# Two steps' value rows weighed by one VectorE instruction, the products written over the keys, and the mark of a chunk's first node made by ScalarE, in a fused graph-attention stage on one core

## The chip, the cores and the metric

The kernel runs on one core of a Trainium2 chip, as one program. The metric is the device time of one execution in microseconds (us). Before the change the median of three runs is 5581.06 us, the lowest 5578.73 and the highest 5584.89.

## The reference, cut to what matters

Two layers of a graph network on 6250 nodes and 200,000 edges sorted by destination, 256 features. The first layer is attention over the incoming edges with 8 heads, the second a relational layer. The change touches only the first:

```python
h = maximum(layernorm(x), 0)
Q, K, V = h @ Wq, h @ Wk, h @ Wv                       # (6250, 8 heads, 32)
score = einsum('ehd,ehd->eh', Q[dst], K[src]) / sqrt(32)
score = score + relu(efeat @ W1 + b1) @ W2 + b2        # edge MLP
m = segment_max(score, dst); ex = exp(score - m[dst])
denom = segment_sum(ex, dst)
out = segment_sum((ex / denom[dst])[:, :, None] * V[src], dst)
x = x + out.reshape(n, 256) @ Wo + bo
```

## The kernel before, in words

The program has several stages one after another: index preparation, projections (Q stays in SBUF, rows of keys and values go to DRAM as kv_d), the fused attention stage (function attend), the messages and gates of the second layer, and its gather and sum. attend is the stage of the change.

Edges come in groups of 256 (two slices of 128, one edge a partition each). A step handles one group against one block of 128 nodes; there are 832 steps, cut into chunks of R = 8. Four groups make a quad of the edge MLP; there are 196 quads, so the MLP ends 48 steps before the steps do. One loop body (body(i), written once for each engine) issues 16 steps, or two chunks; u is the position in it, and u % 8 the step within a chunk. Each engine's order is fixed by that body, and engines meet only through semaphores.

What a step s issues in iteration u of the body:

- GpSimd gathers the two slices of key and value rows of the step into one of 16 slots of kv_rows by indirect DMA (L1006), once the slot's earlier step has been summed.
- ScalarE makes, from distances (Abs, then Relu of one minus it), the selection matrix pickT of step s+3 (L1043, L1049) and the destination matrix onehot of step s-11 (L1056 twice, L1063), and takes the MLP's results out of PSUM (L1021, L1026, L1033).
- TensorE runs select for step s+1 (L1143: the queries of its edges into one of two PSUM banks p_q, after the product of step s-1 has been read), in the iterations 0 to 3 of a chunk one part of the softmax work of the chunk before (score L1155, L1157; up L1162, L1163; down L1167 to L1169; turn_drop L1174), then its part of the MLP (L1122, L1131, L1115; none in iterations 3 and 7), then add_up of step s-12 (L1183: the segment sums of the weighed value rows).
- VectorE runs dot for step s (L1233 multiplies queries and keys into the tile prod, L1238 sums them by head into dots), put in iteration 7 (L1288), then in iterations 0, 1 and 2 one part of the softmax work (scans L1246, L1248; chain L1264 to L1281, ten short instructions on one partition; drop L1294 to L1302), then weigh of step s-11 (L1308: 2 x 264 value elements times the edge's weight by head, in place) and add of step s-12 (L1326: the sums added to the accumulator; before the first of a chunk also rescale, L1316).

The online softmax runs once a chunk: running maxima along the chunk's edges (scans), carried over its steps (chain), subtracted from the scores (drop), turned back to one edge a partition (turn_drop), exponentiated by ScalarE into wgt and scale (weights, L1070 and L1073, in iteration 3). From then on, from iteration 3 of one chunk to iteration 2 of the next, the eight steps are weighed and summed. first_node (L1266) marks, on one partition, which of 128 nodes is the chunk's first; down multiplies it with fall to spread the fall of the maximum.

hold (L62) is a semaphore wait followed by an increment of a counter on the same engine. The constants LATE = R + 3 = 11 and the body's order set all these distances.

Of the kernel before, what the change touches and what calls it, by code (L numbers as in the profile page):

```python
# [16 lines left out]
ALU = mybir.AluOpType  # L17
ACT = mybir.ActivationFunctionType
AX = mybir.AxisListType

P = 128
# [767 lines left out]
LATE = R + 3  # L789
PICKS = 4  # L790
HOTS2 = 2
PASSES = STEPS // SLOTS


def attend(nc, t, q, att, edge_attr, w1, b1, w2, b2, kv_d, mlp_d, dstrow_d, pens_d, line_d, src_d):
    ctx, sb, ps, sem = phase(nc)
    RH = R * H
    with ctx:
# [14 lines left out]
        rows = sb("kv_rows", [P, SLOTS, 2, KV])  # L813
        prod = sb("prod", [P, 2, D])
        dots = sb("dots", [P, 2, 2, R, H])
# [14 lines left out]
        newmax = sb("newmax", [1, H])  # L830
        fall = sb("fall", [1, H])
        first_node = sb("first_node", [1, P])
        ends = sb("ends", [RH, 2])
        wgt = sb("wgt", [P, 2, 2, R, H])
        scale = sb("scale", [P, H])
# [41 lines left out]
        line_done = sem("line_done")  # L877
        line_down = sem("line_down")
        ends_link = sem("ends_link")
        drop_done = sem("drop_done")  # L880
# [137 lines left out]
        def _(act):  # L1018
# [47 lines left out]
            def weights(c, x):  # L1066
                act.wait_ge(drop_turned, c + 1)
                if not first(c):
                    act.wait_ge(scaled, c)
                nc.scalar.activation(scale[:, :], p_scale, ACT.Exp).then_inc(scale_ready, 1)  # L1070
                if not (isinstance(c, int) and c < 2):
                    act.wait_ge(weighed, R * (c - 1))
                nc.scalar.activation(wgt[:, x, :, :, :].rearrange("p k r h -> p k (r h)"),  # L1073
                                     p_back.rearrange("p (k e) -> p k e", k=2), ACT.Exp).then_inc(wgt_ready, 1)

            def body(i):
                for u in range(SLOTS):
                    s = SLOTS * i + u
                    m = U * i + u // U
                    c = 2 * i + u // R - 1  # L1080
                    if is_step(s + 3):
                        measure(s + 3, (u + 3) // U % 2, (u + 3) % U, 2 * i + (u + 3) // (2 * U))
                    if is_step(s - LATE):
                        measure_dst(s - LATE)
                    if is_quad(m + 1):
                        if u % U < 2:
                            take_hidden(m + 1, u % U)
                        elif u % U == 2:
                            take_mlp(m + 1)
                    if u % U == 3 and is_quad(m + 2):  # L1090
                        take_ef(m + 2)
                    if is_step(s + 3):
                        pick(s + 3, (u + 3) % PICKS)
                    if is_step(s - LATE):
                        hot(s - LATE, (u - LATE) % HOTS2)
                    if u % R == 3 and is_chunk(c):
                        weights(c, (u // R - 1) % 2)
# [13 lines left out]
        def _(pe):  # L1111
# [36 lines left out]
            def score(c, x):  # L1148
                pe.wait_ge(emlp_in, 16 * (c + 1))
                hold(pe, place_ready, c + 1, pe_go)  # L1150
                hold(pe, dots_done, R * (c + 1), pe_go)
                if not first(c):
# [12 lines left out]
            def down(c):  # L1165
                hold(pe, line_done, c + 1, pe_go)
                nc.tensor.transpose(p_ends[:, 0:1], before[:, :], t["ident"][0:1, 0:1])  # L1167
                nc.tensor.transpose(p_ends[:, 1:2], after[:, :], t["ident"][0:1, 0:1])
# [7 lines left out]

            def add_up(s, u):
                pe.wait_ge(hot_ready, s + 1)
                pe.wait_ge(weighed, s + 1)
                if not (isinstance(s, int) and s < 2):  # L1180
# [6 lines left out]
            def body(i):  # L1187
                for u in range(SLOTS):
# [24 lines left out]
                    if is_step(s - LATE - 1):  # L1213
                        add_up(s - LATE - 1, u - LATE - 1)

# [11 lines left out]
        def _(dve):  # L1227
            def dot(s, u, n, x):
                dve.wait_ge(q_done, s + 1)
                dve.wait_ge(gathered[u], 32 * (n + 1))  # L1230
                if not first(s):
                    dve.wait_ge(dots_done, s)
                nc.vector.tensor_tensor(prod[:, :, :], p_q[u % 2][:, :].rearrange("p (k d) -> p k d", k=2), rows[:, u, :, 0:D],  # L1233
                                        ALU.mult).then_inc(prod_done, 1)
                dve.wait_ge(prod_done, s + 1)
                if u % R == 0 and not (isinstance(s, int) and s < 2 * R):
                    dve.wait_ge(score_done, n * 2 + u // R - 1)
                nc.vector.tensor_reduce(dots[:, x, :, u % R, :], prod[:, :, :].rearrange("p k (h c) -> p k h c", h=H),  # L1238
                                        AX.X, ALU.add).then_inc(dots_done, 1)

# [8 lines left out]

            LINKS = 9  # L1250

            def chain(c, s0):
                def linked(n, scan=False):
                    if scan:
                        hold(dve, link, LINKS * c + n, dve_go)
                    else:
# [8 lines left out]
                nc.vector.tensor_copy(firstmax[:, :, :], by_head(p_line[:, 0:RH])[:, :, ::-1]).then_inc(link, 1)  # L1265
                nc.vector.tensor_scalar(first_node[:, :], t["iota"][0:1, :], t["dst"][0:1, bass.ds(2 * s0, 1)], None,  # L1266
                                        ALU.is_equal).then_inc(link, 1)
                linked(1, True)
                nc.vector.tensor_tensor_scan(flat(carried), line[:, 0:H * (R + 1)], flat(lastmax), -BIG, ALU.add, ALU.max).then_inc(link, 1)
                linked(2, True)  # L1270
                nc.vector.tensor_tensor_scan(flat(onward), line[:, H * (R + 1):H * (2 * R + 1)], flat(firstmax), -BIG, ALU.add, ALU.max).then_inc(link, 1)
                linked(4)
                nc.vector.tensor_tensor(by_head(before[:, :]), carried[:, :, 0:R], pen(136, R), ALU.add).then_inc(link, 1)
                nc.vector.tensor_copy(lastmax[:, :, 0:1], carried[:, :, R:R + 1]).then_inc(link, 1)
                linked(5)
                nc.vector.tensor_tensor(by_head(after[:, :])[:, :, 0:R - 1], onward[:, :, R - 2::-1], pen(144, R - 1),
                                        ALU.add).then_inc(link, 1)
                linked(6)
                nc.vector.tensor_tensor(newmax[:, :], before[:, 0:H], onward[:, :, R - 1], ALU.max).then_inc(link, 1)
                linked(9)  # L1280
                nc.vector.tensor_tensor(fall[:, :], before[:, 0:H], newmax[:, :], ALU.subtract).then_inc(line_done, 1)  # L1281
# [22 lines left out]
            def weigh(s, u, c, x):  # L1304
                if u % R == 0:
                    dve.wait_ge(wgt_ready, c + 1)
                v = rows[:, u, :, D:KV].rearrange("p k (h c) -> p k h c", h=H)
                nc.vector.tensor_tensor(v, v, wgt[:, x, :, u % R, :].unsqueeze(3).to_broadcast([P, 2, H, HD1]), ALU.mult).then_inc(weighed, 1)  # L1308

# [19 lines left out]
            def body(i):  # L1329
                for u in range(SLOTS):  # L1330
# [6 lines left out]
                    if is_chunk(c) and u % R < 3:  # L1337
                        if u % R == 0:
                            scans(c)
                        elif u % R == 1:  # L1340
                            chain(c, R * c)
                        else:
                            drop(c)
                    if is_step(s - LATE):
                        v = u - LATE
# [498 lines left out]
```

## Time and profile before

| | |
|---|---|
| median of 3 runs | 5581.06 us (5578.73 to 5584.89) |
| profiled execution, device time | 5578.26 us |
| its span, first to last instruction | 5576.5 us |
| mean granted TensorE clock | 0.878 |
| busy over the span: PE / DVE / ACT / POOL | 4808.8 / 3500.7 / 3299.5 / 3249.0 us |
| the same, share | 86% / 63% / 59% / 58% |
| L1308 (weigh) | 832 instructions, 693 ns mean, 576.5 us |
| L1233 (product), L1238 (head sums) | 832 each, 681 and 686 ns mean |
| L1266 (first_node) | 104 instructions, 265 ns mean, 27.5 us |

Times in the rows are microseconds from the start of the span unless marked ns. PE is TensorE's matmul, PEld its weight load, DVE is VectorE, ACT is ScalarE, POOL is GpSimd. "Busy" is the union of an engine's records in a stretch. Records of neighbouring instructions overlap: one starts while the one before still finishes, so the room that an instruction takes on its engine is the distance to the next start, which is shorter than its duration. An idle time stands in brackets at the end of a timeline line, with what ended it. fp32 matmuls are recorded as two instructions each. The names shelf and p_soft stand for SBUF and PSUM areas that several tiles share: L1326's shelf is the accumulator att, p_soft holds the scores and the small results beside them.

### The profile page before, as it was taken

Reading aid. Unit: us, or ns where it says so; the run is one execution under the profiler, and the core shown is the slowest. Engines: PE = TensorE matmul, PEld = TensorE weight load, DVE = VectorE, ACT = ScalarE, POOL = GpSimd, SP = SyncE. Lnnn points to the kernel's source line nnn. Section 1 sums busy time; section 2 is a strip of 40 time slices with the busy share of each in tenths; the row PEclk is TensorE's granted clock in tenths of the full one; section 3 lists DMA queues with packets and bytes.
Section 4 is the critical chain, followed back from the end, with each engine's and each line's share of the span. In section 5 each row is a group of like instructions: output and inputs, shape, how many; then the busy total and the mean of one; then the engine's idle time right before and its main releaser. Section 6 shows DMA issues by size and latency. Waiting matters only on the chain. (4 is left out here: it accounts for less than half of the span.)

```text
span 5576.5 us, 110596 instructions
## 1 busy us (share of the span) xinstructions
PE 4808.8 (86%) x21476; PEld 2762.5 (50%) x21477; DVE 3500.7 (63%) x8094; ACT 3299.5 (59%) x8030; POOL 3249.0 (58%) x3312
## 2 busy tenths in 40 slices
PE   8899999999999999999799999877777767766666
PEld 5455555555555555555444444444444444444443
DVE  6599999999999999999933333333333333333334
ACT  3588888888888888888644444333333333333333
POOL 0266666666666666666600000177777777777776
PEclk9999999999999999999999999966666676677777
DMA  4577777777777777777644444433333333333335
GB/s 138 165 226 224 228 225 224 228 225 224 228 225 224 228 225 225 228 224 223 181 142 141 142 141 140 135 106 105 106 105 105 105 105 106 105 105 105 105 105 141
DMA packets 551967, 929.49 MB, mean 167 GB/s; under 512 B 112846, under 2 KB 361824, under 8 KB 551905
## 3 DMA queue, kind: packets, MB, share of 16 engines
q0 software_dynamic: 208384, 648.75, 40.9%
q1 hardware_dynamic: 343520, 280.03, 15.7%
q8 instruction: 25, 0.41, 0.0%
q14 instruction: 38, 0.30, 0.0%
HBM read 795.60 MB, written 132.88 MB: 166 GB/s over the span
## 5 line engine op out<-in xcount | busy, mean ns | idle before, releaser
L1006 POOL DMA_INDIRECT kv_rows<-kv_d,idx x1664 | 1716.1, 1031 | 844.2 <-issue 464.2
L1767 PE MATMUL m_sums<-m_rows,m_oh 128*128 x3328 | 1399.8, 570 | 580.8 <-ACT m_rows L1748 507.5
L1704 POOL DMA_INDIRECT m_rows<-msg_d,m_idx x1568 | 1487.3, 949 | 507.3 <-issue 471.5
L1748 ACT ACTIVATE m_rows<-m_rows,m_norm 128x256 f32<-128x256 f32 x1568 | 710.8, 500 | 1268.2 <-DMA m_rows<-msg_d,m_idx 1268.2
L1767 PEld LDWEIGHTS m_sums<-m_rows,m_oh 128*128 128x128 f32 x3328 | 842.8, 277 | 1137.9 <-issue 1013.5
L1790 DVE TENSOR_TENSOR agg<-agg,m_sums 128x256 f32 x832 | 350.5, 421 | 1298.1 <-PE m_sums L1767 1294.3
L1183 PE MATMUL sums<-kv_rows,onehot 128*128 128x264 f32 x3328 | 946.2, 407 | 29.1 <-issue 15.5
L1183 PEld LDWEIGHTS sums<-kv_rows,onehot 128*128 128x128 f32 x3328 | 568.7, 191 | 413.0 <-issue 334.6
L1143 PE MATMUL p_q<-shelf,pickT 128*128 x4992 | 698.1, 275 | 19.7 <-ACT pickT L1049 11.1
L1637 PE MATMUL p_m<-wr,h1T 128*128 128x512 f32 x1568 | 710.5, 596 | 0.0
L1026 ACT ACTIVATE hid<-p_hid,b1s 128x512 f32<-128x512 f32 x784 | 496.3, 684 | 334.2 <-PE p_hid L1122 334.2
L1143 PEld LDWEIGHTS p_q<-shelf,pickT 128*128 128x128 bf16 x4992 | 470.9, 98 | 255.0 <-issue 112.5
L1238 DVE TENSOR_REDUCE dots<-prod 128x16 f32<-128x512 f32 x832 | 570.9, 686 | 33.2
L1233 DVE TENSOR_TENSOR prod<-p_q,kv_rows 128x512 f32<-128x512 f32 x832 | 566.4, 681 | 29.7 <-PE p_q L1143 19.7
L1308 DVE TENSOR_TENSOR kv_rows<-kv_rows,wgt 128x528 f32<-128x528 f32 x832 | 576.5, 693 | 2.6 <-ACT wgt L1073 2.6
L1056 ACT ACTIVATE far_dst<-t_iota,t_dst 128x128 f32<-128x128 f32 x1664 | 570.8, 394 | 0.4
L1478 POOL TENSOR_TENSOR x_res<-x_res,bos 128x256 f32<-128x256 f32 x49 | 35.5, 725 | 761.4 <-DMA x_res<-in_x_dram 723.8
L1525 DVE TENSOR_SCALAR msg<-p_m,gate 128x256 f32<-128x256 f32 x392 | 171.7, 480 | 457.8 <-PE p_m L1637 455.2
L1063 ACT ACTIVATE onehot<-far_dst,t_one 128x256 f32<-128x256 f32 x832 | 418.1, 503 | 53.3 <-PE sums L1183 52.7
L1122 PE MATMUL p_hid<-efT,w1s 64*128 64x512 f32 x1568 | 444.5, 644 | 0.8 <-ACT efT L1021 0.8
L1326 DVE SCALAR_TENSOR_TENSOR shelf<-shelf,t_keep,sums 128x264 f32 x832 | 401.7, 483 | 65.1 <-PE sums L1183 33.3
L1637 PEld LDWEIGHTS p_m<-wr,h1T 128*128 128x128 f32 x1568 | 287.4, 191 | 285.7 <-issue 283.2
(193 smaller groups left out, 4413.0 us busy)
## 6 DMA issues: line engine op xcount, KB each, us to landing
msg_d<-msg SPq DMA_DIRECT2D x196, 512.0 KB, 2.9
dsts<-dstrow_d SPq DMA_DIRECT2D x208, 256.0 KB
ef_raw<-in_edge_attr_dram SPq DMA_DIRECT2D x195, 256.0 KB
kv_rows<-kv_d,idx POOLq DMA_INDIRECT x1664
m_rows<-msg_d,m_idx POOLq DMA_INDIRECT x1568, 2.8
kv_d<-kvo SPq DMA_DIRECT2D x49, 260.0 KB, 2.1
pens<-pens_d SPq DMA_DIRECT2D x104, 96.2 KB
emlp<-mlp_d SPq DMA_DIRECT2D x104, 64.0 KB
```

The lines of the kernel that those rows point to most:

```text
L1006: pool.indirect_dma_start(rows[:, u, k, :], None, kv_d[:, :], bass.IndirectOffsetOnAxis(idx[:, half, c:c + 1], 0)).then_inc(gathered[u], 16)
L1026: nc.scalar.activation(hid[:, k, :, :], p_hid[k][:, :].rearrange("p (g e) -> p g e", g=U), ACT.Relu, bias=b1s[:, half:half + 1]).then_inc( ...
L1056: nc.scalar.activation(far_dst[:, k, :], t["iota"][:, :], ACT.Abs, scale=-1.0, bias=t["dst"][:, bass.ds(2 * s + k, 1)]).then_inc(fard_read ...
L1143: last = nc.tensor.matmul(p_q[u % 2][:, k * D:(k + 1) * D], pickT[:, u % PICKS, k * P:(k + 1) * P], q[:, bass.ds(b, 1), part * D:(part + 1 ...
L1183: last = nc.tensor.matmul(sums[u % 2][:, 0:KV - D], onehot[:, u % HOTS2, k, :], rows[:, u % SLOTS, k, D:KV], start=(k == 0), stop=(k == 1))
L1233: nc.vector.tensor_tensor(prod[:, :, :], p_q[u % 2][:, :].rearrange("p (k d) -> p k d", k=2), rows[:, u, :, 0:D], ALU.mult).then_inc(prod_ ...
L1238: nc.vector.tensor_reduce(dots[:, x, :, u % R, :], prod[:, :, :].rearrange("p k (h c) -> p k h c", h=H), AX.X, ALU.add).then_inc(dots_done, 1)
L1308: nc.vector.tensor_tensor(v, v, wgt[:, x, :, u % R, :].unsqueeze(3).to_broadcast([P, 2, H, HD1]), ALU.mult).then_inc(weighed, 1)
L1637: last = nc.tensor.matmul(p_m[c % 4][:, :], hT[:, s, half, :], wr[:, half, 2 * c:2 * c + 2, :], start=(half == 0), stop=(half == 1))
L1704: pool.indirect_dma_start(rows[:, u, k, :], None, msg_d[:, :], bass.IndirectOffsetOnAxis(idx[:, u // HALF, c:c + 1], 0)).then_inc(gathered ...
L1748: last = nc.scalar.activation(rows[:, u, k, :], rows[:, u, k, :], ACT.Copy, scale=norm[:, bass.ds(2 * g + k, 1)])
L1767: last = nc.tensor.matmul(sums[u % BANKS][:, 0:D], onehot[:, u % HOTS, k, :], rows[:, bass.ds(slot, 1), k, :].rearrange("p a d -> p (a d)" ...
```

## The change

- weigh handles two steps with one instruction (WEIGHS = 2): 4 x 264 elements, issued where u - 11 is even, that is in the iterations 1, 3, 5 and 7 of a chunk, for the steps s-11 and s-10. wgt has its slices inside the steps so that two steps' weights lie side by side, and ScalarE writes it in that order. TensorE's add_up and ScalarE's weights count pairs.
- dot writes the products over the keys in kv_rows and the tile prod is gone, with the wait for the reduction before; the head sums stay one step an instruction (DOTS = 1).
- chain loses the comparison that made first_node (L1266). ScalarE makes it by first_of in iteration 0 of a chunk (Abs, then Relu, on 1 x 128), and TensorE's down has one more hold for it.

```diff
...
 PICKS = 4
+DOTS = 1
+WEIGHS = 2
 HOTS2 = 2
...
         rows = sb("kv_rows", [P, SLOTS, 2, KV])
-        prod = sb("prod", [P, 2, D])
         dots = sb("dots", [P, 2, 2, R, H])
...
         fall = sb("fall", [1, H])
+        far_first = sb("far_first", [1, P])
         first_node = sb("first_node", [1, P])
         ends = sb("ends", [RH, 2])
-        wgt = sb("wgt", [P, 2, 2, R, H])
+        wgt = sb("wgt", [P, 2, R, 2, H])
         scale = sb("scale", [P, H])
...
         line_down = sem("line_down")
+        far1_ready = sem("far_first_ready")
+        first_ready = sem("first_node_ready")
         ends_link = sem("ends_link")
...
                 if not (isinstance(c, int) and c < 2):
-                    act.wait_ge(weighed, R * (c - 1))
-                nc.scalar.activation(wgt[:, x, :, :, :].rearrange("p k r h -> p k (r h)"),
-                                     p_back.rearrange("p (k e) -> p k e", k=2), ACT.Exp).then_inc(wgt_ready, 1)
+                    act.wait_ge(weighed, R // WEIGHS * (c - 1))
+                nc.scalar.activation(wgt[:, x, :, :, :].rearrange("p r k h -> p k r h"),
+                                     p_back.rearrange("p (k r h) -> p k r h", k=2, h=H), ACT.Exp).then_inc(wgt_ready, 1)
+            def first_of(c):
+                if not first(c):
+                    act.wait_ge(first_ready, c)
+                nc.scalar.activation(far_first[:, :], t["iota"][0:1, :], ACT.Abs, scale=-1.0,
+                                     bias=t["dst"][0:1, bass.ds(2 * R * c, 1)]).then_inc(far1_ready, 1)
+                act.wait_ge(far1_ready, c + 1)
+                if not first(c):
+                    act.wait_ge(line_down, c)
+                nc.scalar.activation(first_node[:, :], far_first[:, :], ACT.Relu, scale=-1.0,
+                                     bias=t["one"][0:1, 0:1]).then_inc(first_ready, 1)
...
                         hot(s - LATE, (u - LATE) % HOTS2)
+                    if u % R == 0 and is_chunk(c):
+                        first_of(c)
                     if u % R == 3 and is_chunk(c):
...
                 hold(pe, place_ready, c + 1, pe_go)
-                hold(pe, dots_done, R * (c + 1), pe_go)
+                hold(pe, dots_done, R // DOTS * (c + 1), pe_go)
                 if not first(c):
...
                 hold(pe, line_done, c + 1, pe_go)
+                hold(pe, first_ready, c + 1, pe_go)
                 nc.tensor.transpose(p_ends[:, 0:1], before[:, :], t["ident"][0:1, 0:1])
...
-            def add_up(s, u):
+            def add_up(s, u, batch):
                 pe.wait_ge(hot_ready, s + 1)
-                pe.wait_ge(weighed, s + 1)
+                pe.wait_ge(weighed, batch + 1)
                 if not (isinstance(s, int) and s < 2):
...
                     if is_step(s - LATE - 1):
-                        add_up(s - LATE - 1, u - LATE - 1)
+                        add_up(s - LATE - 1, u - LATE - 1, SLOTS // WEIGHS * i + (u - LATE - 1) // WEIGHS)
...
                 dve.wait_ge(gathered[u], 32 * (n + 1))
-                if not first(s):
-                    dve.wait_ge(dots_done, s)
-                nc.vector.tensor_tensor(prod[:, :, :], p_q[u % 2][:, :].rearrange("p (k d) -> p k d", k=2), rows[:, u, :, 0:D],
+                keys = rows[:, u, :, 0:D]
+                nc.vector.tensor_tensor(keys, p_q[u % 2][:, :].rearrange("p (k d) -> p k d", k=2), keys,
                                         ALU.mult).then_inc(prod_done, 1)
-                dve.wait_ge(prod_done, s + 1)
-                if u % R == 0 and not (isinstance(s, int) and s < 2 * R):
-                    dve.wait_ge(score_done, n * 2 + u // R - 1)
-                nc.vector.tensor_reduce(dots[:, x, :, u % R, :], prod[:, :, :].rearrange("p k (h c) -> p k h c", h=H),
-                                        AX.X, ALU.add).then_inc(dots_done, 1)
+                if (u + 1) % DOTS == 0:
+                    a, r = u + 1 - DOTS, (u + 1 - DOTS) % R
+                    dve.wait_ge(prod_done, s + 1)
+                    if r == 0 and not (isinstance(s, int) and s < 2 * R):
+                        dve.wait_ge(score_done, n * 2 + u // R - 1)
+                    nc.vector.tensor_reduce(dots[:, x, :, r:r + DOTS, :].rearrange("p k r h -> p r k h"),
+                                            rows[:, a:u + 1, :, 0:D].rearrange("p s k (h c) -> p s k h c", h=H),
+                                            AX.X, ALU.add).then_inc(dots_done, 1)
...
-            LINKS = 9
-            def chain(c, s0):
+            LINKS = 8
+            def chain(c):
                 def linked(n, scan=False):
...
                 nc.vector.tensor_copy(firstmax[:, :, :], by_head(p_line[:, 0:RH])[:, :, ::-1]).then_inc(link, 1)
-                nc.vector.tensor_scalar(first_node[:, :], t["iota"][0:1, :], t["dst"][0:1, bass.ds(2 * s0, 1)], None,
-                                        ALU.is_equal).then_inc(link, 1)
                 linked(1, True)
...
                 nc.vector.tensor_tensor_scan(flat(onward), line[:, H * (R + 1):H * (2 * R + 1)], flat(firstmax), -BIG, ALU.add, ALU.max).then_inc(link, 1)
-                linked(4)
+                linked(3)
...
-                linked(9)
+                linked(8)
                 nc.vector.tensor_tensor(fall[:, :], before[:, 0:H], newmax[:, :], ALU.subtract).then_inc(line_done, 1)
...
             def weigh(s, u, c, x):
-                if u % R == 0:
+                r = u % R
+                if r == 0:
                     dve.wait_ge(wgt_ready, c + 1)
-                v = rows[:, u, :, D:KV].rearrange("p k (h c) -> p k h c", h=H)
-                nc.vector.tensor_tensor(v, v, wgt[:, x, :, u % R, :].unsqueeze(3).to_broadcast([P, 2, H, HD1]), ALU.mult).then_inc(weighed, 1)
+                v = rows[:, u:u + WEIGHS, :, D:KV].rearrange("p s k (h c) -> p (s k) h c", h=H)
+                w = wgt[:, x, r:r + WEIGHS, :, :].rearrange("p r k h -> p (r k) h").unsqueeze(3).to_broadcast([P, 2 * WEIGHS, H, HD1])
+                nc.vector.tensor_tensor(v, v, w, ALU.mult).then_inc(weighed, 1)
...
                         elif u % R == 1:
-                            chain(c, R * c)
+                            chain(c)
                         else:
                             drop(c)
-                    if is_step(s - LATE):
+                    if is_step(s - LATE) and (u - LATE) % WEIGHS == 0:
                         v = u - LATE
...
```

## Rows read from the trace of the kernel before

**Rows 1.** Tile view of kv_rows: least/median/longest ns, first and last start.
```profile
L1183 PE MATMUL sums<-kv_rows,onehot x3328: 386/386/780, 264.8 to 2798.9; 128*128 128x264 f32 x196
```

**Rows 2.** Busy time of each engine by stretch, granted clock, DMA share, GB/s.
```profile
1000.00:1400.00 400.00, 386.35 (x2438) 225.88 (x2437) 379.78 (x812) 344.00 (x878) 269.71 (x262) 1.00 0.79 226
...
2625.00:2650.00 25.00, 20.16 (x96) 12.45 (x95) 24.20 (x53) 16.41 (x46) 16.72 (x17) 0.86 0.76 220
```

**Rows 3.** Groups of instructions from 1000 to 1400 us: busy, mean ns, idle before.
```profile
L1056 ACT ACTIVATE far_dst<-t_iota,t_dst 128x128 f32<-128x128 f32 x260 | 89.3, 395 | 0.0
...
L1326 DVE SCALAR_TENSOR_TENSOR shelf<-shelf,t_keep,sums 128x264 f32 x130 | 62.8, 483 | 10.4 <-PE sums L1183 5.1 <-issue 3.7
...
L1174 PE MATMUL p_soft<-t_ident,fwd 64*128 64x64 f32 x32 | 6.7, 290 | 6.8 <-DVE fwd L1302 6.8
```

**Rows 4.** Timeline of PE, 1000 to 1026 us: start, us, instruction, idle before it.
```profile
1000.67 0.86 PE L1143 MATMUL p_q<-shelf,pickT 128*128 x6
1001.45 1.13 PE L1122 MATMUL p_hid<-efT,w1s 64*128 64x512 f32 x4
...
1008.69 1.06 PE L1183 MATMUL sums<-kv_rows,onehot 128*128 128x264 f32 x4
...
1018.25 1.16 PE L1183 MATMUL sums<-kv_rows,onehot 128*128 128x264 f32 x4
1019.24 0.82 PE L1143 MATMUL p_q<-shelf,pickT 128*128 x6
1019.99 0.19 PE L1167 MATMUL p_soft<-t_ident,before 1*64 1x1 f32 x1
...
1023.56 0.42 PE L1174 MATMUL p_soft<-t_ident,fwd 64*128 64x64 f32 x2 [0.42 <-DVE fwd L1302]
1024.13 1.13 PE L1183 MATMUL sums<-kv_rows,onehot 128*128 128x264 f32 x4
1025.29 0.89 PE L1143 MATMUL p_q<-shelf,pickT 128*128 x6
```

**Rows 5.** Timeline of DVE, 1000 to 1026 us.
```profile
1009.90 0.49 DVE L1326 SCALAR_TENSOR_TENSOR shelf<-shelf,t_keep,sums 128x264 f32 x1 [0.28 <-PE sums L1183]
1010.31 0.68 DVE L1233 TENSOR_TENSOR prod<-p_q,kv_rows 128x512 f32<-128x512 f32 x1
...
1011.82 0.69 DVE L1308 TENSOR_TENSOR kv_rows<-kv_rows,wgt 128x528 f32<-128x528 f32 x1
1012.44 0.47 DVE L1326 SCALAR_TENSOR_TENSOR shelf<-shelf,t_keep,sums 128x264 f32 x1
...
1017.98 0.20 DVE L1264 COPY lastmax<-p_soft 1x64 f32<-1x64 f32 x1
...
1018.24 0.26 DVE L1266 TENSOR_SCALAR first_node<-t_iota,t_dst 1x128 f32<-1x128 f32 x1
1018.43 0.29 DVE L1269 TENSOR_TENSOR_SCAN carried<-line,lastmax 1x72 f32<-1x72 f32 x1
...
1019.42 0.69 DVE L1308 TENSOR_TENSOR kv_rows<-kv_rows,wgt 128x528 f32<-128x528 f32 x1
1020.07 0.49 DVE L1326 SCALAR_TENSOR_TENSOR shelf<-shelf,t_keep,sums 128x264 f32 x1
...
1023.00 0.42 DVE L1302 TENSOR_TENSOR fwd<-p_soft,top 64x256 f32<-64x256 f32 x1
1023.34 0.69 DVE L1308 TENSOR_TENSOR kv_rows<-kv_rows,wgt 128x528 f32<-128x528 f32 x1
...
1024.36 0.67 DVE L1233 TENSOR_TENSOR prod<-p_q,kv_rows 128x512 f32<-128x512 f32 x1
...
1025.67 0.70 DVE L1308 TENSOR_TENSOR kv_rows<-kv_rows,wgt 128x528 f32<-128x528 f32 x1
```

**Rows 6.** Timeline of ACT, 1000 to 1026 us.
```profile
1018.36 1.27 ACT L1026 ACTIVATE hid<-p_hid,b1s 128x512 f32<-128x512 f32 x2 [0.53 <-PE p_hid L1122]
...
1024.78 0.26 ACT L1073 ACTIVATE wgt<-p_soft 128x128 f32<-128x128 f32 x1
```

More of the change, by code:

```diff
@@ L1271, in chain @@
                 nc.vector.tensor_tensor_scan(flat(onward), line[:, H * (R + 1):H * (2 * R + 1)], flat(firstmax), -BIG, ALU.add, ALU.max).then_inc(link, 1)
-                linked(4)
+                linked(3)
                 nc.vector.tensor_tensor(by_head(before[:, :]), carried[:, :, 0:R], pen(136, R), ALU.add).then_inc(link, 1)
                 nc.vector.tensor_copy(lastmax[:, :, 0:1], carried[:, :, R:R + 1]).then_inc(link, 1)
-                linked(5)
+                linked(4)
                 nc.vector.tensor_tensor(by_head(after[:, :])[:, :, 0:R - 1], onward[:, :, R - 2::-1], pen(144, R - 1),
                                         ALU.add).then_inc(link, 1)
-                linked(6)
+                linked(5)
                 nc.vector.tensor_tensor(newmax[:, :], before[:, 0:H], onward[:, :, R - 1], ALU.max).then_inc(link, 1)
-                linked(9)
+                linked(8)
                 nc.vector.tensor_tensor(fall[:, :], before[:, 0:H], newmax[:, :], ALU.subtract).then_inc(line_done, 1)
```

## The prediction

> **What bounds the kernel now.** The whole change lies in the fused attention stage, whose segment sums run from 264.8 to 2798.9 us [rows 1]; the other half of the program is untouched, so I read this stage alone. First the table of busy time by stretch. In 400 us of its steady part VectorE is busy 379.78 us and TensorE 386.35 us, ScalarE 344 us and GpSimd 270 us [rows 2]. So no engine has the stage to itself: VectorE and TensorE are both all but full, and what counts is how they hand work to each other. The last stretches differ: once the edge MLP is finished (from about 2625 us) VectorE is busy 24.20 of 25 us and TensorE only 20.16 [rows 2]: VectorE alone bounds it.
>
> Next the groups of instructions of the same 400 us, with their idle time. The stretch holds 16 chunks of 8 steps. VectorE's add L1326 waits 5.1 us in all for TensorE's sums, 0.3 us a chunk. TensorE's turning of the dropped scores, L1174, waits 6.8 us for VectorE's subtraction L1302, 0.42 us in each of 16 chunks [rows 3]. Each engine waits for the other once a chunk, at different places. That makes a loop, which I follow in the timelines, naming an instruction by its function and step in the chunk (0 to 7; "select 4" is the one TensorE issues in its iteration 4).
>
> 1. TensorE runs without a stop from select 4 at 1000.67 to sums 6 at 1008.69 [rows 4]: 8.02.
> 2. Add 6 waits for these sums and starts at 1009.90 [rows 5]: 1.21. The product of step 7 follows at 1010.31: 0.41.
> 3. From there VectorE is saturated (products, reductions, weighs, adds, scans, line chain, drop) up to L1302 at 1023.00 [rows 5]: 12.69.
> 4. TensorE turns the result at 1023.56 (0.56), starts sums 3 at 1024.13 (0.57), and select 4 at 1025.29 (1.16) [rows 4].
>
> Together 24.62 us, which is select 4 to select 4. The last leg has a little air: sums followed by a select takes 0.99 where nothing holds the select (1018.25 to 1019.24), and here it took 1.16 [rows 4]. Select 4 also needs the product of step 3, at 1024.36 [rows 5], 0.93 before it: that second route sets its start, and the route through the drop is 0.17 behind. Both are nearly equal, which matters below.
>
> **The change, part by part.** Slots are counted start to start, since VectorE's records overlap.
>
> *Weighing two steps at once.* A weigh of 528 elements holds VectorE for 0.62 (1011.82 to 1012.44), in the chain's step 0.65 (1019.42 to 1020.07). The 256-element subtraction holds it for 0.34 (1023.00 to 1023.34) [rows 5]. The difference is 0.28 for 272 elements, about 1.02 ns each, so 528 more elements cost 0.54 and a pair takes 1.16 against 1.24: 0.08 saved a pair, 0.32 a chunk. Bounds: a pair can't be under 1.09, if the whole part of the record that doesn't grow with elements (0.42 less 256 at 1.02 ns, 0.16) left the slot with one of the two instructions, and 1.24 if nothing is saved. I take 1.16, from slots rather than durations, as slots are what the neighbours feel.
> The Trainium skill (VectorE: DVE Perf Modes, The TRN2 errata) gives an fp32 tensor_tensor (N+151)/0.96 ns and holds that many small tiles pay the fixed latency each; read as throughput, that is 157 ns a pair. It is a rival below.
>
> *Where the weighs lie.* Pairs go out in iterations 1, 3, 5 and 7. Between product 7 and L1302, leg 3, lie the weighs of iterations 7, 0 and 1, which take 0.62 + 0.62 + 0.65 = 1.89. In their place come two pairs, 1.16 + 1.19 = 2.35: the leg grows by 0.46, though the chunk as a whole shrinks, because iteration 2's share is now done ahead of the drop rather than behind it. Up to product 3 the saving is real: four weighs, 2.51, against 2.35.
>
> *first_node leaves VectorE.* Its slot is 0.19 (1018.24 to 1018.43) [rows 5]. The scan behind it waits for the first copy (1017.98, 0.20 long), and at 1018.24 that is only 0.06 past, so the wait that the compare hid may show. Between 0.05 and 0.19 saved; I take 0.15.
>
> *Two ScalarE instructions a chunk in its place.* L1056, the same operation on 128 elements, takes 395 ns [rows 3]; two, the second waiting for the first, make about 0.75. Their cover is the 0.53 that ScalarE idles before hid at 1018.36 [rows 6]; 0.2 is left and is carried along ScalarE, which has no idle time from there to the weights (1024.78 plus 0.26 [rows 6]): ready about 1025.24 instead of 1025.04. Weigh 3 starts at 1025.67 [rows 5] and would start 0.31 earlier, 1025.36. It still just finds them. Should it be late by a few tenths, behind it are add 3 and the products of 4 and 5, where VectorE has the air that shows as the 0.28 wait before add 6: nothing is lost until that is used up. The mark itself is needed by TensorE's down (before row at 1019.99 [rows 4]), and is written some 2.5 us ahead. If the two cost double, weigh 3 waits 0.6 and the sums of step 4 begin to be late.
>
> *One more hold on TensorE in down*, a wait and an increment, no row prices it: nothing to 0.1. Cover: the 0.42 that TensorE waits before L1174 soon after. Its place in the queue is ahead of mlp_out and the sums of step 2; VectorE takes those behind the whole drop. I take 0.
>
> *add_up waits for a pair.* Sums 4 need pair 3, which ends about 2.55 after product 3 starts; they start about 2.8 after it (select 4 at 0.93 plus its 0.78 plus the hidden layer). It fits, by 0.2 or more. Sums 6 need pair 5, over 1 us old.
>
> *Products over the keys, wait dropped, weights' layout, link count.* Same elements in runs of 256 and the product starts with no idle time before it now: 0. Bounds minus 0.02 to plus 0.02 a step. No DMA is added or moved; the gather of a slot is released by the sums as before, SP's index load by the product as before.
>
> *Sum.* Leg 3: +0.46 - 0.15 = +0.31. The 0.17 of air on the last leg is used: +0.14. Select 4, no longer held, needs 0.75 to its successor as at 1019.24 to 1019.99, not 0.78 as at 1000.67 to 1001.45 [rows 4]: +0.11 a chunk. The 104 chunks are 97 with the MLP and 7 without. 97 x 0.11 = +10.7 us. In the 7, VectorE gains 0.32 + 0.15 = 0.47 each: -3.3 us. Net **+7.4 us** on the profiled execution of 5578.3 us (its span 5576.5), 5585.7; the median of the three runs is 5581.1, inside which spread (5578.7 to 5584.9) the profiled one lies at the low end, so I put **5587**. The outcome: no difference worth the name, about what a measurement of this kernel can tell from no change being 0.2%, 11 us.
>
> **Rivals.**
> A. *VectorE alone decides* (the change pays). For it: 95% busy, idle only a few tenths a chunk. Against it: the two waits of [rows 3], which close the loop above. It gives 0.47 x 104 = -49 us: 5532. If the drop is less late than I hold (pair at 1.09, the compare's full 0.19), the same loop gives +0.32 - 0.19 - 0.20 = -0.07 a chunk and with the last seven -12: 5569, the border. Chance 0.20 for a gain over 11 us.
> B. *The drop comes late and nothing gives it back* (slower). Place: TensorE's wait at L1174. If 1.16 is what sums after a stall cost and not the hold of select 4, the 0.17 of air does not exist and the leg's +0.31 goes through whole; with the compare's lower end, +0.41. Price: 97 x 0.31 - 3 = +27 us, 5608; at most +37. It decides from a growth of the leg of about 0.15 over the air. For it: TensorE's wait is seen in every chunk. Against: sums have 0.99 to the next at the other place. Chance 0.38 for a loss over 11 us, the upper part of my own sum counted in, since it stands just 4 us under that bound.
> C. *The fixed part counts whole.* By records, 0.16 a pair and 0.265 for the compare: 0.9 a chunk, -94 us, 5484. Slots speak against it (0.62 for a record of 0.70), and TensorE at 386 of 400 us could give no more than 3%. Chance 0.02, inside "faster". By the rule that the Trainium skill (VectorE: DVE Perf Modes, The TRN2 errata) states, each instruction saved is worth its whole fixed term, which is this case.
>
> **How the numbers follow.** Mine, within 11 us: 0.40; A and C 0.22; B 0.38. The range leaves out C and the far end of A below and B's most costly form above: 5548 to 5612.
>
> **What would show it.** Right: L1308 416 times at about 1.24 us each; VectorE's busy time in 400 us down by some 9 us (0.47 of 23.4 a chunk, and longer chunks); TensorE's wait before L1174 up from 0.42 to about 0.7 a chunk, with select 4 right behind sums 3 at 0.99; add 6 still waiting for the sums; chunks of 24.7 in the steady part, 23.5 in the last seven. Wrong: a chunk at 24.2 or less (A), L1174's wait unchanged, or select 4 still 1.16 behind sums 3 with chunks at 24.9 (B). A wait of VectorE on the weights before pair 3 would show ScalarE short of cover, one of TensorE before sums 4 the pair too late.

## The result and the profile after

The changed kernel takes 5630.66 us (median of 4, 5627.46 to 5630.84), the one before 5580.44 in the same runs (5578.73 to 5584.89): ratio 1.0087, 95% interval 1.0074 to 1.01. It is 50 us slower; the forecast was 5587, with a range up to 5612. The profiled execution took 5630.84 us, 52.6 more than the one before. From its page:

```profile
span 5629.0 us, 110767 instructions
...
PE 4812.4 (85%) x21476; PEld 2756.0 (49%) x21477; DVE 3475.7 (62%) x7574; ACT 3358.9 (60%) x8238; POOL 3338.7 (59%) x3312
...
L1329 DVE TENSOR_TENSOR kv_rows<-kv_rows,wgt 128x1056 f32<-128x1056 f32 x416 | 518.0, 1245 | 2.7 <-ACT wgt L1077 2.7
...
L1347 DVE SCALAR_TENSOR_TENSOR shelf<-shelf,t_keep,sums 128x264 f32 x832 | 401.6, 483 | 131.5 <-PE sums L1202 73.2
```

VectorE has 520 instructions less (8094 before) and 25 us less work, and the kernel is slower: the time went into waiting. The tile view of kv_rows says in which stage:

```profile
L1202 PE MATMUL sums<-kv_rows,onehot x3328: 386/386/807, 267.0 to 2850.0; 128*128 128x264 f32 x196
```

The last sums come 51.1 us later than in [rows 1], the first 2.2 us later: all but some 1.5 us of the difference arises up to the end of the fused stage, and 48.9 us of it between its first sums and its last. (The lines have moved: select is L1161, sums L1202, turn_drop L1193, the product L1251, the subtraction that ends the drop L1321, weigh L1329, add L1347.) The busy time of its steady part, to be held against [rows 2], and the groups with their idle time, against [rows 3]:

```profile
1000.00:1400.00 400.00, 380.00 (x2396) 221.13 (x2396) 368.54 (x719) 347.09 (x894) 276.92 (x256) 1.00 0.77 222
```

```profile
L1347 DVE SCALAR_TENSOR_TENSOR shelf<-shelf,t_keep,sums 128x264 f32 x128 | 61.8, 483 | 20.5 <-PE sums L1202 10.7 <-issue 5.0 <-DVE shelf L1337 3.7
...
L1193 PE MATMUL p_soft<-t_ident,fwd 64*128 64x64 f32 x32 | 6.7, 290 | 15.9 <-DVE fwd L1321 15.9
```

Both engines are less busy. TensorE waits 15.9/16 = 0.99 us a chunk for the drop, where it waited 0.42 and I had forecast 0.7. And the idle time before the add has doubled, from 10.4 to 20.5 us, in part for "issue", that is for nothing that the profile shows the engine to wait for. Where that lies is seen in VectorE's timeline of one chunk of the changed kernel:

```profile
1029.30 0.68 DVE L1251 TENSOR_TENSOR kv_rows<-p_q,kv_rows 128x512 f32<-128x512 f32 x1
...
1030.81 1.24 DVE L1329 TENSOR_TENSOR kv_rows<-kv_rows,wgt 128x1056 f32<-128x1056 f32 x1
1031.98 0.47 DVE L1347 SCALAR_TENSOR_TENSOR shelf<-shelf,t_keep,sums 128x264 f32 x1
...
1034.60 0.68 DVE L1269 TENSOR_TENSOR_SCAN top<-pens,fwd 64x256 f32<-64x256 bf16 x1
1035.37 0.49 DVE L1347 SCALAR_TENSOR_TENSOR shelf<-shelf,t_keep,sums 128x264 f32 x1
1035.77 0.68 DVE L1251 TENSOR_TENSOR kv_rows<-p_q,kv_rows 128x512 f32<-128x512 f32 x1
...
1037.22 0.20 DVE L1286 COPY firstmax<-p_soft 1x64 f32<-1x64 f32 x1
1037.56 0.29 DVE L1288 TENSOR_TENSOR_SCAN carried<-line,lastmax 1x72 f32<-1x72 f32 x1
...
1040.15 0.67 DVE L1251 TENSOR_TENSOR kv_rows<-p_q,kv_rows 128x512 f32<-128x512 f32 x1
...
1042.66 0.42 DVE L1321 TENSOR_TENSOR fwd<-p_soft,top 64x256 f32<-64x256 f32 x1
1043.39 0.49 DVE L1347 SCALAR_TENSOR_TENSOR shelf<-shelf,t_keep,sums 128x264 f32 x1 [0.31 <-issue]
1043.80 0.68 DVE L1251 TENSOR_TENSOR kv_rows<-p_q,kv_rows 128x512 f32<-128x512 f32 x1
...
1045.12 1.25 DVE L1329 TENSOR_TENSOR kv_rows<-kv_rows,wgt 128x1056 f32<-128x1056 f32 x1
...
1046.68 0.68 DVE L1251 TENSOR_TENSOR kv_rows<-p_q,kv_rows 128x512 f32<-128x512 f32 x1
```

The pair is as forecast: 1.17 (1030.81 to 1031.98) for 2 x 0.62. But in the even iterations no weigh stands ahead of the add any more. In iteration 4 rescale stands there, and in iteration 6 the add waits for its sums in any case; in the iterations 0 and 2 it does not follow at once: 0.77 behind the scan (1034.60; 0.75 on average), where the weigh used to follow at 0.61; 0.73 behind L1321 (1042.66), where the weigh followed at 0.34 [rows 5]. What stands between them in the code is block_of, a load of the step's block number from SBUF into a register (quoted from add):

```python
def add(s, u, c):
    b = block_of(nc, dve, t, s)
    dve.wait_ge(summed, s + 1)
```

A weigh used to stand ahead of it, and the load ran under the weigh. The trace records each load (TENSOR_LOAD, on the sequencer that hands VectorE its instructions, DVEq), at 0.31 us in the median. Here is the group in the 400 us of the changed kernel, then the one load that falls between L1321 at 1042.66 and the add behind it (answers by the line of the load):

```profile
L784 DVEq TENSOR_LOAD <-t_steps x144: 300/309/317, 999.8 to 1399.1; - x144
```

```profile
L784 DVEq TENSOR_LOAD <-t_steps x1: 302/302/302, 1042.8 to 1042.8; - x1
```

In the kernel before, the same load begins as soon behind L1302 (1023.00):

```profile
L784 DVEq TENSOR_LOAD <-t_steps x1: 302/302/302, 1023.1 to 1023.1; - x1
```

There VectorE had the weigh of 1023.34 to run meanwhile; in the changed kernel it has nothing. One add of the kernel before looks as if it lacked that cover, the one behind rescale:

```profile
1004.00 0.43 DVE L1316 TENSOR_TENSOR shelf<-shelf,scale 128x264 f32 x1
1004.64 0.49 DVE L1326 SCALAR_TENSOR_TENSOR shelf<-shelf,t_keep,sums 128x264 f32 x1 [0.22 <-issue]
```

But this "issue" is not a load: both loads of that iteration (rescale and add load the number each) lie ahead of rescale, and at 1004.00 the sequencer already stands in the wait of this add (L1324), among others for rescale's own result:

```profile
L784 DVEq TENSOR_LOAD <-t_steps x2: 310/312/313, 1002.9 to 1003.4; - x2
L1324 DVEq EVENT_SEMAPHORE  x1: 661/661/661, 1003.8 to 1003.8; - x1
```

The theory that the uncovered loads cost the time I call "lost cover". Its rivals: "lumps" (only the order of long and short iterations matters) and "mark" (ScalarE's two instructions, TensorE's hold or the products over the keys).

### The profile page after: what moved, and what is told of

It reads as the page before. It is cut to its first block and busy times, and to the rows that moved or that the text cites. A ratio compares the mean times of both kernels' runs of the same rounds, so it can differ in the third digit from the quotient of the medians.

```text
span 5629.0 us, 110767 instructions
## 1 busy us (share of the span) xinstructions
PE 4812.4 (85%) x21476; PEld 2756.0 (49%) x21477; DVE 3475.7 (62%) x7574; ACT 3358.9 (60%) x8238; POOL 3338.7 (59%) x3312
## 5 line engine op out<-in xcount | busy, mean ns | idle before, releaser
L1010 POOL DMA_INDIRECT kv_rows<-kv_d,idx x1664 | 1803.9, 1084 | 806.4 <-issue 473.1
L1202 PE MATMUL sums<-kv_rows,onehot 128*128 128x264 f32 x3328 | 953.0, 410 | 16.0 <-ACT onehot L1067 8.0
L1202 PEld LDWEIGHTS sums<-kv_rows,onehot 128*128 128x128 f32 x3328 | 573.2, 192 | 392.7 <-issue 232.8
L1161 PE MATMUL p_q<-shelf,pickT 128*128 x4992 | 705.0, 277 | 13.1 <-ACT pickT L1053 9.3
L1161 PEld LDWEIGHTS p_q<-shelf,pickT 128*128 128x128 bf16 x4992 | 464.0, 98 | 263.5 <-issue 130.9
L1258 DVE TENSOR_REDUCE dots<-kv_rows 128x16 f32<-128x512 f32 x832 | 570.8, 686 | 33.2
L1251 DVE TENSOR_TENSOR kv_rows<-p_q,kv_rows 128x512 f32<-128x512 f32 x832 | 566.2, 681 | 31.1 <-PE p_q L1161 20.7
L1329 DVE TENSOR_TENSOR kv_rows<-kv_rows,wgt 128x1056 f32<-128x1056 f32 x416 | 518.0, 1245 | 2.7 <-ACT wgt L1077 2.7
L1347 DVE SCALAR_TENSOR_TENSOR shelf<-shelf,t_keep,sums 128x264 f32 x832 | 401.6, 483 | 131.5 <-PE sums L1202 73.2
```

What stands on the lines that cost most here:

```text
L1010: pool.indirect_dma_start(rows[:, u, k, :], None, kv_d[:, :], bass.IndirectOffsetOnAxis(idx[:, half, c:c + 1], 0)).then_inc(gathered[u], 16)
L1161: last = nc.tensor.matmul(p_q[u % 2][:, k * D:(k + 1) * D], pickT[:, u % PICKS, k * P:(k + 1) * P], q[:, bass.ds(b, 1), part * D:(part + 1 ...
L1202: last = nc.tensor.matmul(sums[u % 2][:, 0:KV - D], onehot[:, u % HOTS2, k, :], rows[:, u % SLOTS, k, D:KV], start=(k == 0), stop=(k == 1))
L1251: nc.vector.tensor_tensor(keys, p_q[u % 2][:, :].rearrange("p (k d) -> p k d", k=2), keys, ALU.mult).then_inc(prod_done, 1)
L1258: nc.vector.tensor_reduce(dots[:, x, :, r:r + DOTS, :].rearrange("p k r h -> p r k h"), rows[:, a:u + 1, :, 0:D].rearrange("p s k (h c) -> ...
L1329: nc.vector.tensor_tensor(v, v, w, ALU.mult).then_inc(weighed, 1)
```

## The experiments

Several runs fell on chips where the kernel before itself took 6379 to 6474 us, with irregular waits in every stage. One row of the first such kernel shows it (e1_singles, busy time of the steady stretch; TensorE was busy 386 of 400 in [rows 2]):

```profile
1000.00:1400.00 400.00, 343.98 (x2099) 198.09 (x2097) 325.56 (x684) 305.01 (x781) 233.85 (x223) 0.98 0.67 193
```

Tenths of a microsecond a chunk can't be read from their times, so the kernels were run again (f1 is e1, f2 is e3, f3 is e5, f4 is e2, i1 is g1 and h1, i2 is g2 and h2), and only distances between neighbouring starts are used from the first ones.

| kernel | us (median) | before, beside it | ratio, 95% interval | chunk, us |
|---|---|---|---|---|
| changed, again (e6) | 5628.89 | 5580.25 | 1.0088 (1.0071 to 1.0104) | 25.07 |
| pairs alone (f4) | 5631.29 | 5583.23 | 1.0088 (1.0071 to 1.0105) | 25.07 |
| single weighs (f1) | 5574.64 | 5583.23 | 0.9985 (0.9976 to 0.9995) | 24.54 |
| block number early (f2) | 5582.15 | 5583.23 | 0.9999 (0.999 to 1.0009) | 24.59 |
| the same for iteration 2 alone (i2) | 5600.39 | 5580.62 | 1.0037 (1.0021 to 1.0053) | 24.77 |
| pairs and singles (i1) | 5577.78 | 5580.62 | 0.9994 (0.9984 to 1.0004) | 24.58 |
| pairs in even iterations (f3) | 5851.57 | 5583.23 | 1.0477 (1.0459 to 1.0494) | |
| pairs in even iterations, other chip (e5, one run) | 6486.65 | 6379.06 | | |
| on the other chips: e1 / e2 / e3 / e4 | 6393 / 6344 / 6343 / 6380 | 6398.7 | 0.999 / 0.9901 / 0.9902 / 0.9971 | |
| g2 / g1 | 6349 / 6349 | 6393.6 | 0.9911 / 0.9916 | |
| h2 / h1 | 6396 / 6405 | 6473.6 | 0.9876 / 0.9888 | |

A chunk is the mean distance of product 7 to product 7 over 11 or 12 chunks of the timeline from 990 to 1290 us; it is 24.60 in the kernel before.

**Which part it is.** e1 and f1 undo the pairs, e2 and f4 do them alone:

```diff
-WEIGHS = 2
+WEIGHS = 1
```

> The changed kernel with WEIGHS = 1: single weighs again, the products over the keys and the mark by ScalarE stay. Theory 'lost cover' (the weigh of iterations 0 and 2 used to hide the load of the block number that stands ahead of the add; without it the add comes late, 0.14 us in iteration 0 and 0.39 in iteration 2) and the rival 'lumps' (it is only that two weighs ahead of the drop are longer than one): both want the chunk back at 24.6 us and 5572 to 5588 us. Rival 'mark' (the two ScalarE instructions, TensorE's extra hold or the products over the keys cost the time): stays within 10 us of 5630.

> e1_singles once more, for a chip where the kernel before takes 5580 us. 'Lost cover' and 'lumps': 5572 to 5588 us, chunks of 24.5 to 24.65. 'Mark': 5620 to 5638.

> The kernel before with the pairs alone. 'Lost cover' and 'lumps': the whole loss is in it, 5618 to 5638 us, chunks of 25.0. 'Mark': within 10 us of 5580.

> e2_pairs_alone once more. 'Lost cover' and 'lumps': the whole loss, 5618 to 5638 us, chunks of 25.0. 'Mark': 5572 to 5588.

f1 5574.64, f4 5631.29: the pairs carry the whole loss, "mark" falls. What else the change does is a small gain, 0.9985: product 1 to product 2, the iteration of the compare, is 3.81 us before and 3.74 in f1, 0.07 less; the chunk is 0.06 less, 6 us over 104.

**Why the pairs cost.** e3 and f2 keep them and move only the load (rescale and the add behind it now share one, so a chunk has eight loads instead of nine):

```diff
+                    if is_step(s):
+                        multiply(s, u, i, u // R)
+                    if is_step(s - LATE - 1):
+                        b = block_of(nc, dve, t, s - LATE - 1)
                     if is_step(s):
-                        dot(s, u, i, u // R)
+                        head_sums(s, u, i, u // R)
...
-                b = block_of(nc, dve, t, s)
```

(multiply and head_sums are the two halves of dot.)

> The changed kernel with the block number loaded behind the product of the same iteration, ahead of the head sums, instead of ahead of rescale and add. 'Lost cover': the starts of add 0 and add 2 come 0.14 and 0.38 us nearer to the instruction before; product 3 no longer sets select 4, the route through the drop does, with chunks of 24.7: 5590 to 5605 us. 'Lumps': nothing changes, 5622 to 5638, and L1321 to the add of iteration 2 is still 0.72.

> e3_block_early once more. 'Lost cover': 5590 to 5605 us, chunks of 24.7, select 4 set by the route through the drop; 'lumps': 5622 to 5638.

VectorE's and then TensorE's timeline of f2:

```profile
1020.40 0.68 DVE L1271 TENSOR_TENSOR_SCAN top<-pens,fwd 64x256 f32<-64x256 bf16 x1
1021.00 0.45 DVE L1347 SCALAR_TENSOR_TENSOR shelf<-shelf,t_keep,sums 128x264 f32 x1
...
1028.27 0.42 DVE L1323 TENSOR_TENSOR fwd<-p_soft,top 64x256 f32<-64x256 f32 x1
1028.61 0.47 DVE L1347 SCALAR_TENSOR_TENSOR shelf<-shelf,t_keep,sums 128x264 f32 x1
1029.01 0.68 DVE L1251 TENSOR_TENSOR kv_rows<-p_q,kv_rows 128x512 f32<-128x512 f32 x1
```

```profile
1028.84 0.42 PE L1193 MATMUL p_soft<-t_ident,fwd 64*128 64x64 f32 x2 [0.85 <-issue]
1029.18 1.16 PE L1202 MATMUL sums<-kv_rows,onehot 128*128 128x264 f32 x4
1030.18 0.82 PE L1161 MATMUL p_q<-shelf,pickT 128*128 x6
```

The adds follow 0.60 and 0.34 behind, as a weigh would. 48 of the 50 us are gone: "lumps" alone is refuted, and the load's cover is the cause. Behind rescale the add still starts 0.60 later, with 0.18 of "issue" before it, though no load is left there: that wait never was the load's. The time beat my expectation (5590 to 5605) because the chunk came to 24.59, not 24.7. Select 4 now stands 0.99 behind sums 3 and 1.17 behind product 3 (means): the route through the drop sets it, as forecast.

e4 makes the same move in the kernel before:

> The kernel before with the same move of the load. Under 'lost cover' all of its adds but the one behind rescale have a weigh ahead of them, and that one (0.22 us) lies where VectorE has air: 5574 to 5584 us, no difference. If the load costs something everywhere, the chunk shortens by over 0.1 us and the time falls under 5570.

It ran only where the times can't be read this finely (ratio 0.9971, 0.995 to 0.9992, on such a chip). By the distances, its load was all but free everywhere: weigh to add is 0.62 as before where nothing else holds it, and behind rescale, where it was mean 0.645, the least distances are 0.60 to 0.61. The 0.22 that I counted there as the load's is for the most part the wait for rescale, as told above. What the move is worth in time was not settled.

**How the two exposed loads divide.** g2, h2 and i2 move the load for iteration 2 alone (the condition gets "and u % R == 2").

> The changed kernel with the block number loaded early for the add of iteration 2 alone (the one 0.72 us behind L1321). It puts the two exposed loads apart. 'Lost cover': product 3 comes 0.38 us nearer to product 7, the 0.14 of iteration 0 stays and lies ahead of the drop, so the route through the drop takes over with chunks of 24.7 to 24.75: 5592 to 5600 us, between f2_block_early (5582) and the changed kernel (5629). If only one of them ever mattered it would equal one of the two within 4 us.

> g2_block_early_in_2 a last time. Where the kernel before takes 5580 us: 5592 to 5600 us, chunks of 24.7 to 24.75, if both exposed loads count as the loop has it; within 4 us of 5582 or of 5629 if only one of them ever did.

5600.39 (four of its five runs lie between 5596.93 and 5606.79, their median 5599.94; the fifth took 14462 us, and nothing here says why) at chunks of 24.77: the edge of what was expected, and far from both other kernels. Both loads count: 0.30 us a chunk goes with the one, 0.18 more with the other.

**Sum or loop.** g1, h1 and i1 take f2 and leave the last two steps of a chunk single:

```diff
-WEIGHS = 2
+GROUP = {0: 2, 2: 2, 4: 2, 6: 1, 7: 1}
...
```

> f2_block_early with pairs only where they don't lengthen the way to the drop: steps 0 and 1, 2 and 3, 4 and 5 of a chunk in pairs (iterations 3, 5, 7), steps 6 and 7 alone (iterations 1 and 2, one of them behind the drop as in the kernel before). By the loop: 1.82 us of weighing between product 7 and L1321 instead of 2.34, the leg back at 12.6, product 3 sets select 4, chunks of 24.48 to 24.56: 5569 to 5577 us, as f1_singles and no better, though there are three VectorE instructions fewer a chunk. By VectorE's sum: three times 0.08 us fewer a chunk than f1_singles, 5550.

> g1_mixed a last time. By the loop: 5569 to 5577 us, chunks of 24.48 to 24.56. By VectorE's sum: 5550.

5577.78 us, just above what was expected, and chunks of 24.58: within 0.05 of f1, with three VectorE instructions fewer. VectorE's sum, which wanted 5550, falls. That it is not below f1 has a cause in the table of legs below: pair 3 makes product 4 late for select 5, 0.07 us.

**The order turned round.** e5 and f3 set LATE = R + 4 in f2.

> The kernel of e3_block_early with LATE = R + 4: weighing and summing one step later, so that the pairs go out in iterations 0, 2, 4 and 6 and only one pair (iteration 0) lies between product 7 and the drop instead of two. 'Lost cover' plus the loop through VectorE and TensorE: fwd comes 12.3 us behind product 7 (12.69 in the kernel before), product 3 sets select 4 again, 13.9 behind product 7, chunks of 24.5: 5562 to 5576 us where the kernel before takes 5581. Rival 'order does not matter, the DVE sum does': the same time as e3_block_early.

> e5_pairs_even once more. The loop through VectorE and TensorE: product 3 some 13.9 us behind product 7, chunks of 24.5, 5562 to 5576 us, below the kernel before. 'Order does not matter': as f2_block_early.

5851.57, a miss by 280 us, and not for the reason tested. The tile view of kv_rows in f3 has two rows (who waited for it, us and times) that the kernel before has with 371.2 and 9.7:

```profile
  POOL kv_rows L1010: 459.7, 319
  DVE kv_rows L1251: 274.4, 210
```

Summing a step later frees its slot of kv_rows a step later; with 16 slots the gathers then start too late, and the product waits for them 210 times, 274 us in all. So the prefetch of the kernel before has no step to spare. Whether pairs in the even iterations are better with a 17th slot was not tried.

**The chip.** e6 is the changed kernel itself.

> The changed kernel itself once more, because the chips of the first two calls took 6380 to 6399 us for the kernel before where the first chip took 5581. On a chip where the kernel before takes some 5580 us: 5625 to 5635, ratio 1.009. On one where it takes some 6390 us, 'lost cover' says nothing for certain (its 0.5 us a chunk is hidden behind the longer waits of such a chip, and e2_pairs_alone came out at 0.990): between 0.985 and 1.0. Were it 1.009 there as well, e2 and e3 would have differed from it by something other than the chip.

It fell on an undisturbed chip and repeats the result. Where the kernel before takes 6379 us or more, every kernel with pairs in the odd iterations came out 0.8 to 1.2% faster than it, the pairs in the even ones (e5, one run) 1.7% slower, and the single weighs level. Nothing here shows why; it is left open.

## Why the prediction was wrong

The loop that I followed is the right one, and it adds up in every kernel. Its legs, each the mean over 11 or 12 chunks, in us (f4 and e6 differ from the changed kernel by 0.01 at most):

| | before | changed | f1 | f2 | i2 | i1 |
|---|---|---|---|---|---|---|
| product 7 to L1302/L1321/L1323 | 12.65 | 13.26 | 12.59 | 13.08 | 13.26 | 12.55 |
| product 7 to product 3 | 14.01 | 14.39 | 13.94 | 13.81 | 14.00 | 13.90 |
| product 3 to product 4 | 2.33 | 2.89 | 2.33 | 2.88 | 2.88 | 2.88 |
| product 3 to select 4 | 0.94 | 0.94 | 0.94 | 1.17 | 1.17 | 0.94 |
| select 4 to sums 6 | 8.03 | 8.11 | 8.04 | 7.98 | 7.98 | 8.11 |
| sums 6 to product 7 | 1.62 | 1.62 | 1.62 | 1.63 | 1.62 | 1.63 |
| chunk | 24.60 | 25.07 | 24.54 | 24.59 | 24.77 | 24.58 |

Each chunk is the sum of the second, fourth, fifth and sixth rows (changed: 14.39 + 0.94 + 8.11 + 1.62 = 25.06). Where product 3 to select 4 is 0.94, product 3 sets select 4; where it is 1.17, the drop does. Point by point:

- **The pair's price was right**: 1.17 against a forecast of 1.16. So was the reading that the time depends on where the weighs lie. In leg 3, two pairs instead of three singles were to add 0.46: 2 x 1.17 less 0.62, 0.60 and 0.65 is 0.47.
- **The step that failed is "Where the weighs lie"**: I took each weigh's slot out at its full 0.62 and costed the adds that stay at nothing. Behind the scan the add came 0.14 late, behind the drop 0.39. That is 0.53 of VectorE's time a chunk, and f2 shows it as 48 us. The prediction did not name the block load among what stands ahead of the add: it asked what hides each piece of work that was put in, and not what the weigh that was taken away had hidden. The loads, 0.31 us each, were in the trace.
- **The compare saved nothing here**: product 1 to product 2 takes 4.34 on average both with it (f4) and without it (changed), against a forecast of 0.15 less. From the second copy to the scan it is 0.22 and 0.34 in turn from chunk to chunk (1037.22 to 1037.56 is a long one), 0.28 on average, against 0.13 + 0.19 with the compare between; the 0.05 gained is lost again in the links behind, some of which start 0.01 to 0.03 later. Without pairs, f1, it is 0.22 every time, and 0.07 is saved. Why every second chunk has the longer distance with pairs is not shown.
- **Which route decides**: the drop came 0.61 later, not 0.31, and would alone have given 13.26 + 0.56 + 0.35 + 0.99 = 15.16 for select 4; product 3 gives 14.39 + 0.94 = 15.33, since the exposed 0.39 behind L1321 lies on its way only. So the route of the kernel before stayed in charge, and the air of 0.17 was never used.
- **Also missed**: sums 3 had waited for weigh 2 behind the drop (0.57 from turn_drop to sums 3); with pairs that wait is gone (0.35), a gain of 0.22 on the route that does not decide. And pair 3 stretches product 3 to product 4 to 2.89, so that select 5 waits: 0.08, though I had pronounced that stretch free.
- **Sum**: 0.38 + 0.08 + 0.01 (product 3 to select 4, 0.936 and 0.945 before rounding) = 0.47 a chunk. 0.47 x 97 = 46 us. The last seven chunks, from which I took 3.3 us, take 23.9 on average before and 23.8 in the changed kernel (scan to scan), so they give back under 1 us; and the first distance from scan to scan is 26.1 against 23.6, 2.5 us that the sum did not have.
- **Costed right**: the two ScalarE instructions (385 and 401 ns), the hold in down, and the products over the keys cost nothing that shows (f1 is faster than the kernel before).
- **Rivals**: B had the way of the change, TensorE's longer wait at L1193 and its own sign (select 4 still 1.17 behind sums 3, chunks of 24.9 or more), but at most 37 us and by another mechanism: it held that sums after a stall cost 1.16 to the next select, and f2 and i2 have 0.99 there once product 3 no longer holds the select. A fell. C fell too: the records of a pair are 0.14 shorter than two single ones (2 x 693 against 1245 ns), but its slot only 0.07. (Two figures in the rivals are a little off and change nothing: the least slot of a pair is 1.08, not 1.09, and C counted from 5578.3 where A and B count from 5581.) Without the exposed load the change would have come out at 5582, 5 us under my figure and by the route that I described: the missing term is the load.

## What to carry to other kernels

Before an instruction is merged away, look at what stands between it and its successor in the queue: register loads, holds and waits run under a long instruction and appear in no row of busy time as long as it is there. Their price is in the trace all the same: the records of the sequencer, asked for by the line of the load, give its length and its place. An idle time marked "issue" does not give it; the one behind rescale looked like the same load already bare and was a wait for rescale's result. Where a register load can be had earlier, put it behind a long instruction that something waits for anyway; here that gave back 48 of 50 us, but no more than that, because the two engines' loop, not the sum of instructions, sets the chunk. The fastest kernel tried keeps the single weighs and takes only the rest of the change: 5574.64 us, 0.9985 of the kernel before (i1 has 0.9994, and the two intervals overlap).

## What was not expected of the hardware

A register load from SBUF costs up to 0.39 us of VectorE's time, over half a 528-element multiply, if it stands behind an instruction that had itself to wait for its predecessor. There the load began 0.09 to 0.13 us after that instruction's start and took 0.30 to 0.31, and with the register work and the waits behind it the add was ready 0.73 (L1321) to 0.75 us (the scan, mean) after the same start. What of this VectorE feels is what the instruction ahead does not fill: 0.34 is filled by L1321, so 0.39 is lost, and 0.61 by the scan, so 0.14. Behind rescale the changed kernel has 0.65 to 0.68, of which 0.60 stands without a load too. Behind a weigh nothing is lost: weigh to add is 0.60 to 0.62 with the load and without it. That the wait of the instruction ahead is what makes the load late fits these four places and was not tested by itself. The Trainium skill (DMA: Bandwidth & Descriptors, Latency and other measured facts) gives a tensor_load a floor of about 600 ns; the trace does not agree, its loads take 0.31 us in the median (299 to 326 ns from 1000 to 1400 us of the kernel before), and the measurement decides.
